# The last stage's expert units in half batches, with the first half finished in the same pass

## The reference

```
logits = x3 @ Wg.T                      # 8 experts
w      = softmax(logits), the two largest kept and renormed
gu_e   = x3 @ W1[e].T + b1[e]           # 512 columns: 256 u, 256 g
h_e    = u * sigmoid(g) * w_e           # 256 columns
acc    = sum over e of h_e
out    = layernorm(x3 + acc @ Wo.T + bo * sum(w))
```

## Time and profile before

| | us |
|---|---|
| median of 3 runs | 715.69 (713.93 to 716.35) |
| the profiled execution | 717.6 |
| its span | 715.5 |
| PE busy | 590.8 (83%) |
| DVE busy | 435.7 (61%) |
| POOL busy | 427.4 (60%) |
| ACT busy | 277.4 (39%) |
| granted clock of TensorE, mean | 0.862 |

### The profile page before, as it was taken

How to read it: one execution, slowest core, us unless ns; L and a number is a source line. 1 busy time by engine, 2 the same in 40 slices (tenths; PEclk the granted TensorE clock), 3 DMA queues, 4 the chain that set the end, 5 groups by cost and what they waited for, 6 DMA issues and landing times.

```text
span 715.5 us, 10181 instructions
## 1 busy us (share of the span) xinstructions
PE 590.8 (83%) x3201; PEld 469.0 (66%) x3201; DVE 435.7 (61%) x1448; ACT 277.4 (39%) x559; POOL 427.4 (60%) x407
## 2 busy tenths in 40 slices
PE   5998999389299983468998998988998889989783
PEld 4797888235288863356777777766777677767552
DVE  2455777789544446335576666647666776676642
ACT  3465565225122212523445345243362453532230
POOL 6343434618677773842875976856759759434371
PEclk9999899559655555687999999999999999999996
DMA  4697484598022223320300301103003000000000
GB/s 118 176 301 290 171 308 171 191 200 167 24 68 64 64 62 138 136 93 1 119 0 2 133 1 62 72 1 112 20 0 132 0 4 13 0 16 2 0 15 16
DMA packets 47091, 61.96 MB, mean 87 GB/s; under 512 B 12898, under 2 KB 39745, under 8 KB 46018
## 3 DMA queue, kind: packets, MB, share of 16 engines
q1 hardware_dynamic: 44482, 56.15, 24.9%
q0 software_dynamic: 2560, 5.23, 2.5%
HBM read 35.16 MB, written 24.13 MB: 83 GB/s over the span
## 4 chain that ended last, share of the span: by engine, by line
PE 48%; DVE 21%; issue 9%; ACT 8%; POOL 8%; DMA 4%; SPq 1%; DVEq 0%; POOLq 0%; ACTq 0%
PE pair L1193 5%; PE pair L1194 4%; PE pair L1195 4%; PE pair L1425 4%; POOL c_acc L842 4%; DVE c_g L1061 3%; DVE cand L1624 3%; DVE keyT L1626 2%; PE pair L1299 2%; PE pair L1435 2%; PE pair L467 2%; PE pair L1288 2%; PE pair L1275 2%; ACT c_sg L929 2%; PE pair L1293 2%
## 5 line engine op out<-in xcount | busy, mean ns | idle before, releaser
L842 POOL TENSOR_TENSOR c_acc<-c_acc,c_g 128x1024 f32<-128x1024 f32 x56 | 133.6, 2385 | 79.4 <-DVE c_g L1061 78.6
L1061 DVE SCALAR_TENSOR_TENSOR c_g<-pair,c_comb,c_sg 128x256 f32<-128x256 f32 x224 | 96.9, 477 | 63.3 <-ACT c_sg L929 61.6
L929 ACT ACTIVATE c_sg<-pair 128x512 f32<-128x512 f32 x128 | 76.2, 596 | 149.4 <-PE pair L1195 149.4
L1193 PE MATMUL pair<-c_w_hi,c_x3h 128*128 128x512 f32 x256 | 112.2, 438 | 9.6 <-DVE c_g L1061 7.3
L1194 PE MATMUL pair<-c_w_lo,c_x3h 128*128 128x512 f32 x256 | 102.5, 400 | 0.0
L1195 PE MATMUL pair<-c_w_hi,c_x3l 128*128 128x512 f32 x256 | 102.4, 400 | 0.0
L1193 PEld LDWEIGHTS pair<-c_w_hi,c_x3h 128*128 128x128 f32 x256 | 49.5, 193 | 30.0 <-DVE c_g L1061 20.7
L1195 PEld LDWEIGHTS pair<-c_w_hi,c_x3l 128*128 128x128 f32 x256 | 49.2, 192 | 11.6
L1194 PEld LDWEIGHTS pair<-c_w_lo,c_x3h 128*128 128x128 f32 x256 | 49.6, 194 | 7.4
L1509 POOL DMA_INDIRECT rows_all<-token_rows,tok_row x32 | 31.2, 976 | 12.6 <-issue 8.2
L1514 POOL DMA_INDIRECT routed_rows<-x1T_all,dest_row x32 | 32.3, 1008 | 9.8 <-issue 8.5
(11 more groups left out here) (326 smaller groups left out, 1497.7 us busy)
## 6 DMA issues: line engine op xcount, KB each, us to landing
routed_rows<-rows_all SPq DMA_DIRECT2D x8, 2048.0 KB
c_c<-routed_rows SPq DMA_DIRECT2D x7, 2048.0 KB, 8.0
token_rows<-a_xw SPq DMA_DIRECT2D x8, 384.0 KB, 3.1
a_x<-in_L_attn_x SPq DMA_DIRECT2D x8, 256.0 KB, 3.3
base_all<-a_xw SPq DMA_DIRECT2D x8, 256.0 KB, 3.5
c_c<-routed_rows SPq DMA_DIRECT2D x4, 512.0 KB, 5.2
out<-c_outb SPq DMA_DIRECT2D x8, 256.0 KB, 5.3
wgu_late<-in_L_ffn_w_gate SPq DMA_DIRECT2D x4, 480.0 KB, 7.1
```

The lines of the kernel that those rows point to most:

```text
L842: g.tensor_tensor(acc, acc, b[f"g{e % 2}"][:, :, :], ALU.add).then_inc(s["acc"], 1)
L929: a_.activation(b[f"sg{q % 2}"][:, :, :], self.pair[q % 2][:, :, H1:2 * H1], SIG).then_inc(s["sig"], 1)
L1061: ins = v.scalar_tensor_tensor(out=dst[:, j, :], in0=self.pair[q % 2][:, x, 0:H1], scalar=b[f"comb{uf}"][:, j * E1 + e:j * E1 + e + 1], in ...
L1193: t.matmul(dst, w_hi, x_hi, start=start, stop=False)
```

## The change

The units are numbered by half batches: unit q is expert q % 8 on the tiles of half q // 8, so that the first two tiles have all eight experts by place 7. `g` becomes a ring of four buffers of two tiles, and POOL adds 14 times 128x512 a batch instead of 7 times 128x1024. The end of a batch is split by halves: the first half's transposes, output product, sum, norm and store stand at places 10, 11, 11 and 15 of the same pass, the second half's at 1, 2, 3 and 5 of the next. Each half needs four transposes and one ACT copy, four of the eight 128x128 products, and half of DVE's block; the column sum of the weights (`csum`) is taken once, in the first half's block. POOL's first-half `rstd` stands between adds 11 and 12.

```diff
-AT = dict(zT=0, accT=1, out=3, gate=2, y4=4, quads=3, gate2=3, v=4, outb=6, sim=6, off=7, atd=7, av=8, w=9, x3=10, x3T=12, lg=13, y=7, z=11)
+AT = dict(zT=0, accT=(10, 1), out=(11, 2), gate=2, y4=(11, 3), quads=3, gate2=3, v=4, outb=(15, 5), sim=6, off=7, atd=7, av=8, w=9, x3=10, x3T=12, lg=13, y=7, z=11)
...
-            k(f"outb{u}", [P, NT * D]); k(f"sgt{u}", [P, L]); k(f"sg{u}", [P, 2, H1]); k(f"g{u}", [P, NT, H1])
+            k(f"outb{u}", [P, NT * D]); k(f"sgt{u}", [P, L]); k(f"sg{u}", [P, 2, H1])
             k(f"acc{u}", [P, NT, H1]); k(f"comb{u}", [P, NT * E1]); k(f"csum{u}", [P, NT])
+        k("g", [P, 4, 2, H1])
...
-        k("accT", [P, 2, L])
+        k("accT", [P, 2 * 2 * P])
...
+                sp.wait_ge(s["outb"], 2 * t + 2)
+                self.store_out(sp, t, ua, 1)
+            if f is not None:
+                sp.wait_ge(s["outb"], 2 * f + 1)
+                self.store_out(sp, f, ur, 0)
...
+        src = self.b[f"outb{u}"][:, :].rearrange("p (j d) -> p j d", d=D)
+        j = slice(2 * half, 2 * half + 2)
+        sp.dma_start(dst[:, j, :], src[:, j, :]).then_inc(self.out_stored[u], 16)
...
+        def rstd_f(t, half):
+            n = 2 * t + (half + 1)
+            rstd("f", n, "rf_step", n, "rs_f", slice(2 * half, 2 * half + 2))
+
+        def add_experts(f, uf, *which):
+            for i in which:
+                half, e = i // 7, i % 7 + 1
+                pool.wait_ge(s["g"], 16 * f + (8 * half + e + 1))
+                if e >= 2:
+                    pool.wait_ge(s["acc"], 14 * f + i)
+                acc = b[f"acc{uf}"][:, 2 * half:2 * half + 2, :]
+                g.tensor_tensor(acc, acc, b["g"][:, (2 * uf + i) % 4, :, :], ALU.add).then_inc(s["acc"], 1)
...
             if f is not None:
-                add_expert(f, uf, 1)
+                add_experts(f, uf, 0, 1)
             if t is not None:
-                rstd("f", t + 1, "rf_step", t + 1, "rs_f")
+                rstd_f(t, 1)
...
             if f is not None:
-                add_expert(f, uf, 2)
+                add_experts(f, uf, 2, 3)
...
             if f is not None:
-                add_expert(f, uf, 3)
+                add_experts(f, uf, 4, 5, 6)
...
             if a is not None:
                 rstd("a", a + 1, "rs_step", a + 1, "rs_a")
             if f is not None:
-                add_expert(f, uf, 4)
-                add_expert(f, uf, 5)
-                add_expert(f, uf, 6)
-                add_expert(f, uf, 7)
+                add_experts(f, uf, 7, 8, 9, 10, 11)
+                rstd_f(f, 0)
+                add_experts(f, uf, 12, 13)
 
...
-                if t is not None and q in (AT["accT"], AT["accT"] + 1):
-                    h = q - AT["accT"]
-                    act.wait_ge(s["accT_mm"], 2 * t + (h + 1))
-                    a_.copy(b["accT"][:, h, :], bank[4][:, :]).then_inc(s["accT"], 1)
+                for n, half in ((f, 0), (t, 1)):
+                    if n is not None and q == AT["accT"][half]:
+                        act.wait_ge(s["accT_mm"], 2 * n + (half + 1))
+                        a_.copy(b["accT"][:, :], bank[4][:, :]).then_inc(s["accT"], 1)
...
         def unit(f, uf, q):
 
-            e, jj = divmod(q, 2)
+            half, e = divmod(q, E1)
+            i = 7 * half + e - 1
             dve.wait_ge(s["sig"], 16 * f + (q + 1))
-            if jj == 0 and e >= 3:
-                dve.wait_ge(s["acc"], 7 * f + (e - 2))
-            if jj == 0 and e == 1 and not first(f):
-                dve.wait_ge(s["acc"], 7 * f)
-            dst = b[f"acc{uf}"] if e == 0 else b[f"g{e % 2}"]
+            if e and (i >= 4 or not first(f)):
+                dve.wait_ge(s["acc"], 14 * f + (i - 3))
             for x in range(2):
-                j = 2 * jj + x
-                ins = v.scalar_tensor_tensor(out=dst[:, j, :], in0=self.pair[q % 2][:, x, 0:H1], scalar=b[f"comb{uf}"][:, j * E1 + e:j * E1 + e + 1],
+                j = 2 * half + x
+                dst = b["g"][:, (2 * uf + i) % 4, x, :] if e else b[f"acc{uf}"][:, j, :]
+                ins = v.scalar_tensor_tensor(out=dst, in0=self.pair[q % 2][:, x, 0:H1], scalar=b[f"comb{uf}"][:, j * E1 + e:j * E1 + e + 1],
                                              in1=b[f"sg{q % 2}"][:, x, :], op0=ALU.mult, op1=ALU.mult)
             ins.then_inc(s["g"], 1)
...
+        def half_sum(t, ut, half):
+
+            csum, T = b[f"csum{ut}"], bank[4]
+            at = 5 * t + 3 * half
+            if half == 0:
+                v.tensor_reduce(csum[:, :], b[f"comb{ut}"][:, :].rearrange("p (j e) -> p j e", e=E1), AX.X, ALU.add).then_inc(s["bo4"], 1)
+                dve.wait_ge(s["bo4"], at + 1)
+                at = at + 1
+            dve.wait_ge(s["out_mm"], 2 * t + (half + 1))
+            v.memset(self.landing(), 0.0)
+            tiles = range(2 * half, 2 * half + 2)
+            for j in tiles:
+                c = slice(j * D, (j + 1) * D)
+                ins = v.scalar_tensor_tensor(out=T[:, c], in0=k["bo_bc"][:, :], scalar=csum[:, j:j + 1], in1=T[:, c], op0=ALU.mult, op1=ALU.add)
+            ins.then_inc(s["bo4"], 1)
+            dve.wait_ge(s["bo4"], at + 1)
+            c = slice(2 * half * D, 2 * (half + 1) * D)
+            v.tensor_tensor(T[:, c], b[f"x3{ut}"][:, c], T[:, c], ALU.add).then_inc(s["bo4"], 1)
+            dve.wait_ge(s["bo4"], at + 2)
+            v.memset(self.landing(), 0.0)
+            stats("f", T, 2 * t + (half + 1), tiles)
+
+        def half_norm(t, ut, half):
+            dve.wait_ge(s["rs_f"], 2 * t + (half + 1))
+            dve.wait_ge(self.out_stored[ut], 16 * (t - ut) + 16)
+            norm("f", b[f"outb{ut}"], bank[4], b["rs_f"], s["outb"], range(2 * half, 2 * half + 2))
...
+                if t is not None and q == AT["y4"][1]:
+                    half_sum(t, ua, 1)
+                if t is not None and q == AT["outb"][1]:
+                    half_norm(t, ua, 1)
+                if f is not None and q == AT["y4"][0]:
+                    half_sum(f, uf, 0)
...
+                if f is not None and q == AT["outb"][0]:
+                    half_norm(f, uf, 0)
...
         def up(f, uf, q):
 
-            e, jj = divmod(q, 2)
+            half, e = divmod(q, E1)
             if q >= 2 or not first(f):
...
             for x in range(2):
-                j = 2 * jj + x
+                j = 2 * half + x
                 tok = slice(j * P, (j + 1) * P)
...
-                if t_ is not None and q in (AT["accT"], AT["accT"] + 1):
-                    h = q - AT["accT"]
-                    if h == 0:
-                        pe.wait_ge(s["acc"], 7 * t_ + 7)
-                        if not first(t_):
-                            pe.wait_ge(s["outb"], t_)
-                    else:
-                        pe.wait_ge(s["accT"], 2 * t_ + 1)
-                    for j in range(NT):
-                        ins = t.transpose(bank[4][:, j * P:(j + 1) * P], b[f"acc{ua}"][:, j, h * P:(h + 1) * P], ident[:, :])
-                    ins.then_inc(s["accT_mm"], 1)
-                if t_ is not None and q == AT["out"]:
-
-                    pe.wait_ge(s["accT"], 2 * t_ + 2)
-                    for j in range(NT):
-                        for h in range(2):
-                            ins = t.matmul(bank[4][:, j * D:(j + 1) * D], b["accT"][:, h, j * P:(j + 1) * P], k["woT"][:, h, :], start=(h == 0), stop=(h == 1))
-                    ins.then_inc(s["out_mm"], 1)
+                for n, un, half in ((f, uf, 0), (t_, ua, 1)):
+                    if n is not None and q == AT["accT"][half]:
+                        pe.wait_ge(s["acc"], 14 * n + 7 * (half + 1))
+                        if half or not first(n):
+                            pe.wait_ge(s["outb"], 2 * n + half)
+                        for x in range(2):
+                            for h in range(2):
+                                c = slice((2 * x + h) * P, (2 * x + h + 1) * P)
+                                ins = t.transpose(bank[4][:, c], b[f"acc{un}"][:, 2 * half + x, h * P:(h + 1) * P], ident[:, :])
+                        ins.then_inc(s["accT_mm"], 1)
+                    if n is not None and q == AT["out"][half]:
+                        pe.wait_ge(s["accT"], 2 * n + (half + 1))
+                        for x in range(2):
+                            j = 2 * half + x
+                            for h in range(2):
+                                c = slice((2 * x + h) * P, (2 * x + h + 1) * P)
+                                ins = t.matmul(bank[4][:, j * D:(j + 1) * D], b["accT"][:, c], k["woT"][:, h, :], start=(h == 0), stop=(h == 1))
+                        ins.then_inc(s["out_mm"], 1)
```

52 lines of the change are left out of this document (12 added, 40 removed).

## The result

The changed kernel takes 704.41 us (median of 4 runs, 702.14 to 706.81) against 716.02 us for the kernel before (4 runs, 713.93 to 718.52): a ratio of 0.983, with a 95% interval of 0.980 to 0.986. It is faster by 11.6 us where 18.9 were forecast. The profiled execution took 702.37 us with a span of 700.6. It is one of the two shorter ones of its four, while the profiled one of before (717.6, span 715.5) was one of the longer ones: the two traces lie 14.9 us apart, 3.3 more than the medians.

The account below looks back on a forecast made before the run. No engine is full; a chain of waits between engines bounds each pass. Passes -10.8, clock +1.1, last pass and tail -9.2: -18.9 from the 715.7 us median gives 697 us; own range 692 to 702, wider range 689 to 708.

Parts of the forecast that it names:

- only the tail gains: Rival, chance 0.22: hole at place 13 halves the clock in all seven passes; passes gain 2 us, tail 9.2; 704.5 us.
- Place 4's block to place 3, the hole before `sim`: Half block fits DVE's idle time at place 3, ending PE's 1.98 us wait; place 1 transposes to `sim` 2.6 us less.
- The half block at place 11: Between units 11 and 12 on DVE's chain without slack: 2.0 us, adding 1.8 us up to the last unit.
- The shorter add at place 1: POOL's add behind the last unit, awaited by PE at place 1, shrinks from 2.39 to 1.29 us: 1.1 us less.
- The clock: Half clock moves from before `sim` to before place 13's gating product: 1.65 us in two of three passes, net +1.1 us.
- f7 up to unit 7: Last expert pass, start to unit 7: hole, slow clock, transposes and half product go, some waits come; -3.5 us.
- Places 10 and 11 in f7: Last expert pass: half block at place 11 starts unit 12 about 1.3 us late, PE's waits absorb some; +1.0 us.
- The last add: POOL's final add, last expert pass: 1.1 us shorter, 0.4 returned by the first half's rstd between adds; -0.7 us.
- Transposes to norm: Tail, from last transposes to norm's end: only half a batch remains, 7.1 us instead of 13.06; -6.0 us.
- The last store: Tail, norm's end to span's end: left at 4.1 us; an estimated 0.3 us saving from halving was not counted.
- POOL and SP: POOL's fourteen short adds, +1.3 us busy per pass, hidden; SP's sixteen stores instead of eight cost nothing.
- ACT holds `c_v`: Slower rival, chance 0.05: ACT's scaled copies delay `c_v`, so removing place 4's block frees nothing; 735 us.

Follow-up runs that it names:

- the fillers: Changed kernel plus fourteen unused 128x128 transposes on PE ahead of its wait for `c_x3l` at place 13; 693.44 us, ratio 0.968 to the kernel before.
- the kernel with place 4: Changed kernel with the first half's block moved from place 11 to 13 and the second half's from 3 to 4; 707.89 us, ratio 0.988.
- The kernel with fillers in the tail: Changed kernel with first block at place 13, its statistics at 14, POOL's half rstd behind add 12, plus 34 unused PE transposes after the last unit; 686.46 us.
- the run without one: Changed kernel keeping the half order of units and short adds, but no batch ends its first half early; 712.88 us, ratio 0.994 to the kernel before.

## Why the prediction was right in direction and 7.6 us off

The measured 704.4 us lay inside the range (689 to 708), outside the forecast's own range of 692 to 702, and where the rival "only the tail gains" had its 704.5. That rival named the right cause (the hole at place 13 in nearly all passes), but its number is met by luck in part: the passes gained 6.9 us, not 2, and the last stretch 7.5, not 9.2, and 3.3 us lie between traces and medians.

- **Place 4's block to place 3, the hole before `sim`: right.** Forecast 12.6 us from the transposes to `sim`, 2.6 less; measured 12.75, 2.5 less. No `sim` wait, and `sim` to `av` at full clock in every pass. That the cover at place 3 is needed is shown too: at place 4 the half block costs 17.3 us over the six intervals, 2.9 a pass, where the text said 1.8.
- **The half block at place 11: right.** +1.8 us on the chain forecast, +1.6 to 1.9 measured, with 2.03 to 2.18 us from the start of the block with `csum` to the next unit.
- **The shorter add at place 1: right.** 1.1 us, measured 0.9 to 1.1 where the clock is full (8.0 for 9.0 in the last of the seven stretches, 8.0 to 8.2 for 9.0 to 9.3 with the fillers).
- **The clock: the term that failed.** I took the new hole to cost what the old one did, 1.65 us in two passes of three, 7.7 us in seven passes against 6.6 removed. The removal came as forecast (6.8). The new hole cost 11.3 us: six of seven passes lost the clock, and three of them 2.5 us each. I took both rates over with the hole's length, how often and how much, and both failed. How often: six of seven instead of two of three. How much: where the slow clock lasted 3.4 us, as behind the old hole, it cost 1.0 to 1.4, less than the 1.65 there; but in three passes it lasted 6.8 us, through units 14 and 15. In these the twelve eight-column matmuls of the gating product take 2.5 us (510.63 to 513.12), against 1.3 at full clock in the kernel with place 4 (414.35 to 415.61). Why it lasted twice as long in three passes no run shows. The bound I gave for this term, +5 for seven cases of 1.65, was of the right size (+4.6), by other cases; the value inside it was not. With this term at its measured size the forecast for the six intervals would have been -10.8 + 4.6 = -6.2; they gained 6.9.
- **f7 up to unit 7: right.** 3.5 us forecast, 3.4 measured. **Places 10 and 11 in f7:** +1.35 instead of +1.0. **The last add** as forecast. The transposes start 2.7 us earlier instead of 3.2.
- **Transposes to norm: 0.5 short.** 7.6 instead of 7.1. I had taken the first round of the earlier trace rows, 0.73 us to ACT's start, for the only one; in the changed kernel it takes 1.15, and the product 2.12 instead of 1.96. The kernel with fillers in the tail shows 6.25 at full clock. The forecast gave all of this to the early half; the run without one takes 11.25 us here, so 1.8 of the 5.4 come with the halves as such.
- **The last store: 0.6 the other way.** From the norm's end to the span's end it is 4.8 us with 128 KB, against 4.1 with 256 KB. By the Trainium skill ("DMA: Bandwidth & Descriptors", Anatomy of one DMA) the part by bytes would have made it an estimated 0.3 us shorter; the measurement decides, and it went the other way. The Trainium skill gives that sum for transfers that GpSimd issues, and this store is issued by SP, so it may not bear on it at all. The same 4.8 us stand in all seven other kernels that store halves, so it isn't chance in one trace; its cause wasn't tested.
- **POOL and SP: right**, hidden. POOL is 1.7 us busier in a pass (36.57 for 34.86), and stands in no new wait of the changed kernel. **ACT holds `c_v`** (the slower rival) and **no change** fell.
- **The median against the trace.** I put the sum on the median, since the trace lay 1.9 us above it. The two longer executions of the changed kernel have spans of 704.7 and 705.1 at a mean clock of 0.846 against 0.852 in the trace; the 3.3 us that the traces overstate fit more passes with a slow stretch in them, but those runs left no trace, so this is argued and not shown.
